# Attention context kept with features on partitions: packed by transfers and scaled by GpSimd in place of TensorE transposes

## What is computed

```python
# x, ctx: (4, 512, 256)
q = split_heads(layernorm(x) @ Wq.T + bq)      # 16 heads of 16
k = split_heads(ctx @ Wk.T + bk)
v = split_heads(ctx @ Wv.T + bv)
attn = softmax(q @ k.T / 4)
c = merge_heads(attn @ v)                      # "the context", 2048 rows of 256
x = x + tanh(g_xattn) * (c @ Wo.T + bo)
h = layernorm(x)
# 8 experts, the best 2 of each token, weighted by a softmax of their logits
moe = sum_k score_k * (silu(h @ fc1[e_k][:, :256]) * (h @ fc1[e_k][:, 256:])) @ fc2[e_k]
shared = (silu(h @ gate_w) * (h @ up_w)) @ down_w
x = x + tanh(g_ffn) * (moe + shared)
```

## Time and profile before

| | us |
|---|---|
| median of 3 runs | 473.4 (473.13 to 475.3) |
| the profiled execution | 472.9 |
| its span, first to last instruction | 471.2 |
| TensorE busy | 461.7 (98%) |
| DVE busy | 338.4 (72%) |
| ACT busy | 255.7 (54%) |
| GpSimd busy | 118.4 (25%) |

### The profile page before, as it was taken

One profiled execution on the slowest core, in us unless ns is written; L12 is line 12 of the kernel. 1 busy time (PEld: TensorE's weight loads), 2 busy tenths in 40 slices (PEclk: granted clock), 3 DMA queues, 4 the chain that ended last, 5 costly groups with the idle time before them and its releaser, 6 DMA issues.

```text
span 471.2 us, 8172 instructions
## 1 busy us (share of the span) xinstructions
PE 461.7 (98%) x2394; PEld 224.7 (48%) x2394; DVE 338.4 (72%) x858; ACT 255.7 (54%) x544; POOL 118.4 (25%) x143
## 2 busy tenths in 40 slices
PE   8999999999999999999999999999999999999997
PEld 8665422333333333333356564675555555555745
DVE  1888897888888888888847876665565656542574
ACT  1664476777777777777766212113676667631110
POOL 5594485000000000000001177640333223332000
PEclk9999999999999999999999999999999999999999
DMA  8668762956564555320000022232332223211931
GB/s 254 219 179 230 184 198 69 198 141 134 136 134 137 135 134 137 92 69 1 3 1 2 0 102 90 91 110 60 92 87 83 85 87 91 80 57 47 362 114 59
DMA packets 47532, 52.80 MB, mean 112 GB/s; under 512 B 8640, under 2 KB 39744, under 8 KB 47488
## 3 DMA queue, kind: packets, MB, share of 16 engines
q1 hardware_dynamic: 42688, 41.75, 33.1%
q0 software_dynamic: 3168, 8.69, 5.1%
q10 hardware_dynamic: 1632, 1.84, 1.2%
HBM read 34.52 MB, written 17.60 MB: 111 GB/s over the span
## 4 chain that ended last, share of the span: by engine, by line
PE 83%; DVE 6%; DMA 5%; SPq 3%; issue 1%; ACT 1%; POOL 1%; ACTq 0%; POOLq 0%; DVEq 0%
PE PS L1329 12%; PE PS L1241 11%; PE PS L1457 11%; PE PS L1504 10%; PE PS L1611 9%; PE PS L1517 6%; PE PS L1630 5%; PE PS L1606 3%; PE PS L1377 3%; PE PS L1292 3%; PE PS L1625 2%; PE PS L1339 2%; DMA X<-in_x_dram 2%; PE PS L1585 2%; PE PS L1593 2%; DMA q_parts<-R 1%
## 5 line engine op out<-in xcount | busy, mean ns | idle before, releaser
L782 DVE TENSOR_REDUCE nmax<-PS 128x1 f32<-128x512 f32 x256 | 161.8, 681 | 14.7 <-PE PS L1241 14.2
L664 ACT ACTIVATE R<-PS 128x512 f32<-128x512 f32 x256 | 133.2, 603 | 38.9 <-PE PS L1457 38.9
L1241 PE MATMUL PS<-R 96*128 96x512 bf16 x256 | 96.0, 381 | 0.7 <-DMA R<-k_parts 0.5
L1457 PE MATMUL PS<-R 98*128 98x512 bf16 x256 | 86.2, 379 | 1.8 <-DMA R<-mparts 1.5
L1329 PE MATMUL PS<-R 128*32 128x512 f32 x512 | 68.2, 605 | 0.0
L552 POOL DMA_INDIRECT token_y<-R,dest x34 | 32.8, 966 | 86.6 <-DVE R L1124 86.3
L1241 PEld LDWEIGHTS PS<-R 96*128 96x128 bf16 x256 | 24.8, 97 | 56.3 <-DVE nmax L782 39.4
L513 POOL TENSOR_TENSOR rstd<-var_eps,minus_half 128x4 f32<-128x4 f32 x4 | 4.1, 1024 | 187.7 <-DVE var_eps L765 187.7
L1611 PE MATMUL PS<-R 128*128 x100 | 47.3, 595 | 1.0 <-ACT R L738 1.0
L1457 PEld LDWEIGHTS PS<-R 98*128 98x128 bf16 x256 | 24.7, 97 | 41.1 <-ACT R L664 20.9
L683 ACT ACTIVATE R<-PS 128x512 f32<-128x512 f32 x16 | 9.6, 597 | 62.0 <-PE PS L1504 62.0
(11 more groups left out here) (173 smaller groups left out, 602.5 us busy)
## 6 DMA issues: line engine op xcount, KB each, us to landing
R<-q_parts SPq DMA_DIRECT2D x96, 64.0 KB, 3.1
R<-k_parts SPq DMA_DIRECT2D x96, 64.0 KB, 3.2
R<-in_fc_w_dram SPq DMA_DIRECT2D x16, 256.0 KB, 3.0
R<-token_y SPq DMA_DIRECT2D x4, 1024.0 KB, 10.2
R<-slot_x SPq DMA_DIRECT2D x25, 129.0 KB, 2.1
k_parts<-R SPq DMA_DIRECT2D x8, 384.0 KB, 3.2
q_parts<-R SPq DMA_DIRECT2D x8, 384.0 KB, 3.6
fc<-in_fc_w_dram SPq DMA_DIRECT2D x16, 128.0 KB, 3.0
```

Of the source, the lines that this page charges most:

```text
L664: nc.scalar.activation(PT[:, kt, j, :], PS[:, (G * (TB * i + kt) + j) % 3, :], ACT.Exp).then_inc(exp_done, 1)
L782: nc.vector.tensor_reduce(nmax[:, i % 2, j * TB + qt:j * TB + qt + 1], PS[:, smax_bank(n), :], AX.X, ALU.max, negate=True).then_inc(max_re ...
L1241: mm(PS[:, smax_bank(n), :], QS[g][0:KS, j, qt * P:(qt + 1) * P], KST[g][0:KS, j, :], start=True, stop=True).then_inc(smax_done, 1)
L1457: mm(PS[:, n % 3, :], KST[g][0:KM, j, kt * P:(kt + 1) * P], QS[g][0:KM, j, :], start=True, stop=True).then_inc(st_done, 1)
```

## The change

The outputs of groups 0 to 13 (`TURNED` = 14) are no longer transposed. SP stores `OT` whole to DRAM and loads the denominator rows, spread over 128 partitions (`store_out`); one group later it loads the 64 feature rows of a group into half of the 128 partitions of `CTX`, so that two groups fill a slab (`load_out`). DVE takes the reciprocals (`scale_of`), SP stores them and loads them back repeated over 16 partitions each (`store_scale`, `load_scale`), and GpSimd multiplies slab by scales (`scale_context`). `out_projection` reads the slabs as they are; they lie in `CH`, in words that the layer norm of the same or a later batch writes afterwards. The last two groups go the old way (`LAST`, `last_transpose`). With it:

- `ctt_first` and three of four `ctt_second` go; `ctx_transpose` shrinks to four transposes.
- The loads of expert weights move from SP to GpSimd (`load_expert`), each behind a wait for the maxima of a group.
- SP's waits for the stored parts of batches 1 to 3 stand ahead of the groups that need them, no longer all ahead of the loop.
- The token numbers in `CH` are written after the projection of their batch, by GpSimd, in `rstd_second`.
- In `tail` everything moves up: the projection of batch 0 to step 0, and so on; `h2_transpose(1)` comes into the loop; DVE's steps are reordered.
- At the start of the slots, two matmuls of the shared part's last product and DVE's additions of its result move in among the first slots, and the softmax of the two scores behind the third.

```diff
+    TURNED = GROUPS - 2
+            def store_out(i):
+                sp.wait_ge(ot_ready, i + 1)
+                sp.dma_start(o_scr[i], OT[i % 2]).then_inc(o_out[i % 2], 16)
+                sp.dma_start(DENS[:, i % 2, :], OT[i % 2][DK:P:P // G, :].rearrange("j (q n) -> j q n", n=G * TB)).then_inc(den_in[i % 2], 16)
+            def load_out(i):
+                g = i % NG
+                sp.wait_ge(o_out[i % 2], times(i))
+                sp.dma_start(CTX[64 * (g % 2):64 * (g % 2 + 1), i // 2, :],
+                             o_scr[i].rearrange("(j d) n -> j d n", j=G)[:, 0:DK, :]).then_inc(ctx_in[i // 2], 16)
+            def store_scale(i):
+                sp.wait_ge(scale_ready, i + 1)
+                sp.dma_start(r_scr[i].rearrange("j (q n) -> (j q) n", n=G * TB), SCALE[:, i % 2, :]).then_inc(scale_out[i % 2], 16)
+            def load_scale(i):
+                sp.wait_ge(scale_out[i % 2], times(i))
+                if i == 0:
+                    sp.wait_ge(v_done, 2 * B)
+                wait(sp, ctx_scaled, i // 2)
+                sp.dma_start(SCALES[64 * (i % 2):64 * (i % 2 + 1), :],
+                             r_scr[i].unsqueeze(1).to_broadcast([G, DK, S])).then_inc(ctx_in[i // 2], 16)
...
-            for b in range(1, B):
-                parts_stored(b)
-
             for i in range(GROUPS):
+                if i and (i + 3) % NG == 0 and i + 3 < GROUPS:
+                    parts_stored((i + 3) // NG)
...
+                if 0 <= i - 1 < TURNED:
+                    store_out(i - 1)
+                if 0 <= i - 2 < TURNED:
+                    load_out(i - 2)
+                    store_scale(i - 2)
+                if 0 <= i - 3 < TURNED:
+                    load_scale(i - 3)
...
+            def scale_context(n):
+                pool.wait_ge(ctx_in[n], 16 * 4)
+                nc.gpsimd.tensor_tensor(CTX[:, n, :], CTX[:, n, :], SCALES, ALU.mult).then_inc(ctx_scaled, 1)
...
+            for i in range(2, GROUPS - 1):
+                if i < 2 + E:
+                    pool.wait_ge(m2_ready, i + 2)
+                    load_expert(i - 2)
+                if i >= 4 and i % 2 == 0:
+                    scale_context((i - 4) // 2)
+            rstd_second(0)
+            rstd_second(1)
+            scale_context(TURNED // 2 - 1)
+            rstd_second(2)
...
             def out_copy(i):
                 act.wait_ge(pv_done, TB * (i + 1))
-                if i >= 2:
-                    act.wait_ge(ot_t, i - 1)
+                if 2 <= i < TURNED + 2:
+                    act.wait_ge(o_out[i % 2], times(i - 2))
+                    act.wait_ge(den_in[i % 2], times(i - 2))
...
+            def scale_of(i):
+                dve.wait_ge(den_in[i % 2], times(i))
+                if i >= 2:
+                    dve.wait_ge(scale_out[i % 2], times(i - 2))
+                nc.vector.reciprocal(SCALE[:, i % 2, :], DENS[:, i % 2, :]).then_inc(scale_ready, 1)
...
@@ DVE, tail
                 if n == 4:
-                    h2t_second(0)
-                    ctt_second(2)
                     normalised(1)
+                    logits_turned(0)
+                    residual(2)
+                    logits(0)
                 if n == 5:
-                    logits_turned(0)
-                    logits(0)
+                    statistics(2)
                     choose(0)
-                    residual(2)
-                    statistics(2)
...
@@ TensorE, tail
                 if n == 0:
-                    ctx_transpose(0)
+                    out_projection(0)
                 if n == 1:
-                    out_projection(0)
+                    out_projection(1, (0,))
                 if n == 2:
-                    ctx_transpose(1)
+                    out_projection(1, (1,))
                 if n == 3:
-                    out_projection(1)
+                    h2_transpose(0)
+                    out_projection(2, (0,))
                 if n == 4:
-                    h2_transpose(0)
-                    ctx_transpose(2)
+                    router(0)
+                    out_projection(2, (1,))
+                    router_rows(0)
                 if n == 5:
-                    router(0)
-                    out_projection(2, (0,))
-                    router_rows(0)
-                    out_projection(2, (1,))
+                    h2_transpose(1)
...
-                    if kt == 1 and i:
+                    if kt == 1 and i > TURNED:
                         out_transpose(i - 1)
...
             values(GROUPS - 1, TB - 1)
-            h2_transpose(1)
             rank(0)
             out_transpose(GROUPS - 1)
...
             load_expert(expert1[0], 0)
-            down(BE - 1, 2)
+            down(BE - 1, TB)
             transpose_rows(0)
-            down_part(BE - 1, IC - 1, 2)
-            down_part(BE - 1, IC - 1, 3)
+            down_part(BE - 1, IC - 1, 0)
+            down_part(BE - 1, IC - 1, 1)
...
+                if j < 2:
+                    down_part(BE - 1, IC - 1, 2 + j)
```

More of the change, by code:

```diff
@@ L304, in ctt, with times @@
         def ctt(b, c):
-            return CTT[:, b % 2, c, :]
+            n = DC * b + c
+            return CTX[:, n, :] if n < TURNED // 2 else CTT
+        def times(i):
+            return 16 * (i // 2 + 1)
         @block.sync
@@ L539, in _ @@
                 nc.gpsimd.tensor_tensor(X[:, t, :], X[:, t, :], tg_bo[:, :], ALU.add).then_inc(x_biased, 1)
-            for b in range(B - 1):
-                rstd_second(b)
+            for j in range(4):
+                pool.wait_ge(qp_out[j], 16 * B)
+            for i in range(2, GROUPS - 1):
[8 more added lines that the diff above has]
+            rstd_second(2)
             scatter(0)
@@ L1109, in _, with scales, slot_result @@
             tabulate_units()
-            for h in range(2):
-                shared_out(1, h)
-            dve.wait_ge(exp_sc, 1)
-            step(nc.vector.tensor_scalar(sc[:, 2, :], sc[:, 1, :], 1.0, None, ALU.add))
-            step(nc.vector.reciprocal(sc[:, 3, :], sc[:, 2, :]))
-            step(nc.vector.tensor_tensor(sc[:, 0, :], sc[:, 1, :], sc[:, 3, :], ALU.mult))
-            step(nc.vector.tensor_scalar(scg[:, 0, :], sc[:, 3, :], tg[:, 1:2], None, ALU.mult))
-            step(nc.vector.tensor_scalar(scg[:, 1, :], sc[:, 0, :], tg[:, 1:2], None, ALU.mult))
-            def slot_result(it, u):
-                dve.wait_ge(y_done, it * UN + u + 1)
-                wait(dve, y_out[u], it * 16)
+            def scales():
+                dve.wait_ge(exp_sc, 1)
+                step(nc.vector.tensor_scalar(sc[:, 2, :], sc[:, 1, :], 1.0, None, ALU.add))
+                step(nc.vector.reciprocal(sc[:, 3, :], sc[:, 2, :]))
+                step(nc.vector.tensor_tensor(sc[:, 0, :], sc[:, 1, :], sc[:, 3, :], ALU.mult))
+                step(nc.vector.tensor_scalar(scg[:, 0, :], sc[:, 3, :], tg[:, 1:2], None, ALU.mult))
+                step(nc.vector.tensor_scalar(scg[:, 1, :], sc[:, 0, :], tg[:, 1:2], None, ALU.mult))
+            def slot_result(j):
+                u = j % UN
+                dve.wait_ge(y_done, j + 1)
+                wait(dve, y_out[u], j // UN * 16)
                 nc.vector.tensor_copy(YE[:, u, :], PS[:, 5 + u, 0:D]).then_inc(y_ready, 1)
@@ L1164, in _ @@
                     destination(j + 1)
+                if j < 2:
+                    shared_out(1, j)
+                if j == 2:
+                    scales()
                 if j >= 2:
-                    slot_result(*divmod(j - 2, UN))
+                    slot_result(j - 2)
                 m, at = divmod(j - (FIRST_MIXED - UN), UN)
@@ L1349, in bank_free @@
                 if kind == "ctx_t":
-                    pe.wait_ge(ctt_ready[part], b + 1)
+                    pe.wait_ge(ctt_ready[part], 1)
                 if kind == "wo":
@@ L1540, in _ @@
             router(1)
-            ctx_transpose(3)
+            last_transpose()
             router_rows(1)
```

128 lines of the change are left out of this document (64 added, 64 removed).

## The result

The changed kernel took 485.8 us (median of 4, 483.4 to 487.1) against 473.8 us of the kernel before (median of 4, 473.1 to 475.3): a ratio of 1.024, 95% interval 1.021 to 1.028. Forecast were 463.8 us and a range of 460.5 to 472. The profiled execution took 487.1 us with a span of 485.4, where 471.2 stood before.

The account below looks back on a forecast made before the run. TensorE was taken to bound the attention loop; 1.0 + 6.6 + 2.5 - 0.5 = 9.6 us off the profiled 472.9 gave 463.3, plus 0.5 for the median of runs 463.8 us (chance 0.60), range 460.5 to 472.

Parts of the forecast that it names:

- What bounds the kernel: Attention loop: TensorE sets the pace, busy 12.00 of 12 us a group, with DVE at 10.7 and ACT at 9.0.
- Part 1: Start of the loop: SP, freed of waits for stored parts, sends group 1's maxima earlier; 1.0 us saved.
- Part 2, the transposes: Loop, groups 0 to 13: 14 blocks of four head-output transposes go, 0.47 us each, 6.6 us saved.
- the transposes were free: Rival, loop: transposes stood in time DVE or ACT needed anyway, so only start and tail count; 470 us, chance 0.04.
- Part 2, GpSimd and SP: Loop: GpSimd's multiplies and weight loads are hidden, SP's new issues fit its slack; cost 0.
- Part 2, the bounds for the DMA engines: Loop: load per engine and group is 9.4 of 11.5 us on 16 engines, 15.2 on four; the first was taken.
- The four-wide bound: Loop: if transfers with outer dimension four use four engines only, those need 15.2 of 11.5 us, which doesn't fit.
- The allowance for late maxima: Loop: 0.5 us lost in the sum to maxima landing late, between 0 and 7 us.
- DMA engines fill up: Slower rival, groups 2 to 9: new row transfers on four engines hold up the maxima, 16 us lost; 480 us, chance 0.14.
- the narrow range: Whole kernel: the forecast's own range, 461 to 467 us, with the ends of the first two terms and of the tail.
- Parts 3 and 4: Last six loop steps and start of the slots: fewer context transposes and moved work bring the slots 2.5 us ahead.
- the tail keeps nothing: Rival, tail: GpSimd's queue delays the chain through DVE and the scatters by 2.5 to 4 us; 467 us, chance 0.11.

Follow-up runs that it names:

- e2: Changed kernel with the expert weight loads back on SP's queue, behind the maxima, instead of GpSimd's: 498.1 us, 1.027 of the kernel before.
- e4: Changed kernel with the maxima issued from ACT's queue, everything else left on SP: 497.0 us, 1.024 of the kernel before.
- e7: Kernel before plus two unused loads in each of groups 1 to 14, 64 rows of 2 KB taken as 4 x 16: 486.1 us, ratio 1.026.
- e8: Kernel before plus two unused loads in each of groups 1 to 14, the first 64 rows of 2 KB: 477.4 us, ratio 1.010.
- e1: Changed kernel with denominators, feature rows and scales read from plain rows, outer dimension 64 or 128 (wrong data): 480.6 us, 0.983 of the kernel before.
- e6: Changed kernel with only feature rows and scales read from 64 plain rows, denominators unaltered (wrong data): 477.4 us, 0.986 of the kernel before.
- m2: Changed kernel with feature rows and scales loaded one head at a time, from GpSimd, then SP for the last four groups: 469.2 us, 0.993 of the kernel before.
- m1: Changed kernel with rows and denominators loaded per head, mostly from GpSimd, and DVE's reciprocals taken after spreading, on 128x512: 499.6 us, 1.032 of the kernel before.

## Why the prediction was wrong, step by step

**What bounds the kernel** held: the loop goes by TensorE as long as its operands are there.

**Part 1** held. SP sent the maxima of group 1 at 67.59, not 70.15, and no wait stands at its first scores. 1.0 us.

**Part 2, the transposes,** held. The value products stand the short distance apart in steps without a wait, also where the head transposes were the earlier trace rows:

```profile
153.41 1.07 PE L1388 MATMUL PS<-R 128*32 128x512 f32 x8
156.25 1.06 PE L1388 MATMUL PS<-R 128*32 128x512 f32 x8
159.09 1.07 PE L1388 MATMUL PS<-R 128*32 128x512 f32 x8
```

2.84 us each. Without the new transfers the ratio was 0.976, where 0.980 had been forecast, so the rival "the transposes were free" is out.

**Part 2, GpSimd and SP,** held in size: the multiply took 1.27 us (1.45 forecast), the four weight issues on GpSimd 0.54 to 0.56 us each (0.97 taken, from the indirect DMA), SP's new issues 0.45 to 0.82 us (0.4 to 0.7), and neither queue was the cause (e2, e4).

**Part 2, the bounds for the DMA engines,** is the step that failed. Both ends were in the prediction, 9.4 of 11.5 us with 16 engines and 15.2 of 11.5 on four, and I wrote "I take the first, since the load of maxima, whose target is a single partition row, already lands in 1.7 us". That row was no evidence. By its 32 packets for 16 rows it is a transfer that uses all engines; it says nothing on one whose source has four as its outer dimension. What the runs showed in its place: taken four-wide, two loads a group made the kernel before 2.6% slower, taken 64 wide 1.0% (e7, e8), and the changed kernel with wide loads fell below the kernel before (e1, e6). The prediction found no row for that form in the trace of before, and the only thing that spoke of it, the rule of the Trainium skill's page, said four. With no row for a form, the bound that speaks against the change should have had at least even weight, and not 0.14.

The arithmetic of the bounds was weak as well. The four-wide bound counts the store of the scales as four wide, but it has 128 rows on both sides; without that it is 4.96 + 32 x 0.058 + 8 x 0.058 = 7.3, and 13.8 of 11.5 us. And both bounds start from the window with a share of 0.54. In the other window of the earlier trace rows, with expert weights, 0.88 x 12 = 10.6 us, and even with 16 engines 13.5 of 11.5. Such sums did not decide the matter either: e7's load is 6.5 + 4.0 = 10.5 of 12 by the same prices, which fits, and it lost 2.6%; m2 ran with shares of 0.80 to 0.85 and lost little.

**The allowance for late maxima,** 0.5 us with an upper end of 7, was the term that took the damage: 15.5 us of waits. It came from landings of 1.6 to 2.9 us as they were before, without the narrow loads beside them. The slack was 0.5 us, so any rise of the landing's tail counted in full; the median went only from 1.7 to 2.2, the longest from 2.9 to 6.4.

**What was not in the sum at all,** in no rival either: the clock. 8.7 us come after the waits, not in them. The rival "DMA engines fill up" was priced at 480 and named the right cause, the shape of the new transfers; that its 16 us of lost time is close to the 15.5 measured is chance, since its arithmetic was another (eight groups each a steady 2.0 us over). The eight waits, of 0.85 to 4.13 us, stood in groups with and without expert weights. With the clock added it would have said 488.7; measured 485.8.

**The range.** Its lower end is a little off by the working's own terms: 463.8 - 0.5 - 2.6 is 460.7, not 460.5, and the narrow range would begin at 459.6, not 461. Neither touches the outcome.

**Parts 3 and 4** held. The ranks of batch 0 waited 1.61 us for DVE (1.8 forecast), the first rows' transposes 0.53 us (under 1), and the first product 0.18 where 0.62 stood:

```profile
280.38 0.41 PE L1470 MATMUL PS<-OHS,before 128*128 128x32 f32 x2 [1.61 <-DVE PRE L1012]
...
332.66 0.41 PE L1642 MATMUL PS<-ident,R 128*128 128x128 f32 x2 [0.53 <-DMA R<-slot_x]
...
336.48 0.69 PE L1668 MATMUL PS<-R 128*128 x1 [0.18 <-ACT R L793]
```

The gain itself: TensorE's last transpose of maxima started at 253.94, at 236.84 before, 17.1 us later; the span is 14.2 longer; so the tail and the slots gave back 2.9, where 2.5 was forecast. The rival "the tail keeps nothing" is out.

**What stays open.** Why chips B and C run the kernel before 2.3 to 2.4% slower. What decides after which waits the clock falls. And why, in the four-wide kernel on D, the packets of the stretch 94 to 106 us take longer on all engines: 1732 packets at a DMA share of 1.04 are 115 ns each, in the 64-wide kernel 2106 at 0.78 are 71 ns. A mean share above 1 also means that packets' times overlap on an engine, so they are not pure work. In this stretch, the one with the 6.47 us wait, it is not a few busy engines among idle ones as at 228 us, and the load on four engines alone does not explain it. That the shape costs is shown; the way from the shape to the late landing is not shown in full.

## What to carry to other kernels

Before a transfer is added, write down the outermost dimension of both its sides and split the bytes over that many engines, not over 16; by the packet counts here four heads outermost is four engines, and one transfer a head with 16 rows was the cure. Then ask which small, urgent transfer shares the engines: its slack, not the mean DMA share, is what the new traffic is paid from, and a queue of its own did not protect it. Price a wait of TensorE inside a dense loop at more than its length, because here the clock came back later than the data after half of the eight waits.

## What the runs showed of the hardware

- The transfer of 4 KB of maxima, normally landed in 1.7 us, took up to 8.8 us with two four-wide loads of 128 KB a group beside it, and up to 4.3 with the same loads 64 wide.
- After some waits of TensorE in this loop its granted clock fell to 0.50 and came back 3 to 7 us later, in the changed kernel after 1.69 us, in e2 already after 1.50; after others it did not fall, up to 2.10 us in the changed kernel and 2.56 in its run on chip C. By the mean clock of the span 15.9 us of waits cost 8.7 us more in this way (changed kernel), 10.2 us (e7) 3.4 us more, 3.6 us (e8) nothing.
- DVE's reciprocal of 128x512 in f32 took 3.33 us, where its reduction of as many elements took 0.68 (m1).
- Mean DMA share misleads in both directions: at 0.2 to 0.4 the maxima were under way and came late by 1.69 us (228.2 to 230.8 us, changed kernel), at 0.80 to 0.85 the kernel with a load for each head lost at most 1.4 us at a time.
